# Audio tower on one core: a new order of calls on all five engines, and the low parts cut in two

## The reference, cut to what matters

```python
def _L0_tok_ref(user_batch, filt, W_k, b_k):      # B=32, L=256, D=128, F=8 -> 248 tokens of 64
    windows = user_batch[:, idx, :]
    out = jnp.einsum('blfd,fd,fdk->blk', windows, filt, W)
    return jax.nn.relu(out + b_k)
...
    q = src @ Wq.T + bq; k = src @ Wk.T + bk; v = src @ Wv.T + bv
    row_mask = (q[:, :, 0] != 0) & (k[:, :, 0] != 0)
    prob = softmax(where(row_mask, q @ k.T / 8, -1e9)); prob = where(row_mask, prob, 0)
    return (prob @ v) @ Wo.T + bo
...
    topk_vals, topk_idx = jax.lax.top_k(x @ Wg + bg + bias, 2)     # 8 experts, 2 chosen
    h = relu(x @ W1[e] + b1[e]); y = h @ W2[e] + b2[e]             # all 8 experts, hidden 128
    out = sum_e combine[:, e] * y[e]
...
h = _L0_tok_ref(x, ...)
h = h + _L0_attn_ref(_layernorm(h), ...)
h = h + _L0_ffn_ref(_layernorm(h), ...)
```

## Time and profile before

| | us |
|---|---|
| median of 3 runs | 327.02 (326.04 to 329.09) |
| the profiled execution, device time | 325.06 |
| its span, first to last instruction | 323.3 |
| mean granted TensorE clock | 0.988 of full speed |

### The profile page before, as it was taken

How to read it: one execution, slowest core, us unless ns; L and a number is a source line. 1 busy time by engine, 2 the same in 40 slices (tenths; PEclk the granted TensorE clock), 3 DMA queues, 4 the chain that set the end, 5 groups by cost and what they waited for, 6 DMA issues and landing times.

```text
span 323.3 us, 5597 instructions
## 1 busy us (share of the span) xinstructions
PE 287.1 (89%) x1486; PEld 188.3 (58%) x1486; DVE 253.1 (78%) x824; ACT 230.7 (71%) x545; POOL 96.6 (30%) x85
## 2 busy tenths in 40 slices
PE   8767879899999989898999999898999997978783
PEld 7545647576565748575665657484756654554340
DVE  2476777979798888889797987888897988886653
ACT  2357687878686977978686969869786869574541
POOL 1112141414234241614142241515142312213113
PEclk9789999999999999999999999999999999999999
DMA  5311215061432525170624334251605133232241
GB/s 176 101 32 34 66 52 139 4 177 31 119 89 83 129 81 128 20 190 4 160 51 105 103 81 129 79 131 37 154 22 140 36 87 90 81 95 80 66 128 31
DMA packets 17248, 28.61 MB, mean 88 GB/s; under 512 B 3265, under 2 KB 13761, under 8 KB 17217
## 3 DMA queue, kind: packets, MB, share of 16 engines
q1 hardware_dynamic: 16928, 27.98, 32.8%
q10 hardware_dynamic: 288, 0.28, 0.2%
HBM read 21.90 MB, written 2.29 MB: 75 GB/s over the span
## 4 chain that ended last, share of the span: by engine, by line
PE 76%; issue 7%; DVE 6%; ACT 3%; DMA 3%; SPq 2%; POOL 1%; POOLq 0%; DVEq 0%; ACTq 0%
PE bank_y L877 15%; PE bank_a L817 11%; PE bank_h L867 10%; PE bank_h L868 8%; PE bank_s L926 4%; PE bank_s L845 4%; PE bank_s L834 4%; PE bank_s L909 3%; PE bank_b L886 3%; PE bank_b L935 2%; PE bank_s L882 2%; PE bank_b L882 2%; PE bank_s L886 2%; PE bank_s L957 2%; PE bank_s L946 2%
## 5 line engine op out<-in xcount | busy, mean ns | idle before, releaser
L380 ACT ACTIVATE hid<-bank_h,col 128x496 f32<-128x496 f32 x128 | 82.3, 672 | 17.4 <-PE bank_h L868 17.1
L867 PE MATMUL bank_h<-xs,w_hi 128*128 128x496 f32 x128 | 59.4, 464 | 9.6 <-issue 7.5
L877 PE MATMUL bank_y<-hid,w_sb 128*64 128x496 f32 x256 | 60.4, 587 | 3.1 <-issue 3.1
L331 POOL TENSOR_TENSOR p<-p,rmask 124x496 f32<-124x496 f32 x32 | 32.4, 1013 | 77.6 <-DVE rmask L585 77.5
L255 POOL TENSOR_TENSOR total<-acc 128x496 f32<-128x496 f32 x16 | 20.0, 1250 | 110.3 <-DVE acc L569 110.3
L569 DVE SCALAR_TENSOR_TENSOR acc<-bank_y,col,cb 128x496 f32<-128x496 f32 x64 | 45.0, 722 | 7.8 <-DMA cb<-weights 6.1
L868 PE MATMUL bank_h<-xs,w_lo 128*128 128x496 f32 x128 | 49.5, 387 | 0.0
L867 PEld LDWEIGHTS bank_h<-xs,w_hi 128*128 128x128 f32 x128 | 24.1, 188 | 27.9 <-issue 24.0
L371 ACT ACTIVATE p<-bank_s,nmax 124x248 f32<-124x248 f32 x64 | 29.4, 469 | 9.7 <-DVE nmax L576 9.7
L877 PEld LDWEIGHTS bank_y<-hid,w_sb 128*64 128x64 f32 x256 | 16.6, 136 | 29.1 <-issue 26.1
L338 POOL TENSOR_TENSOR x_lo<-x,x_hi 128x512 fp32r<-128x512 f32 x16 | 24.4, 1524 | 29.3 <-ACT x_hi L436 29.3
(11 more groups left out here) (105 smaller groups left out, 563.2 us busy)
## 6 DMA issues: line engine op xcount, KB each, us to landing
cb<-weights SPq DMA_DIRECT2D x64, 248.0 KB, 3.9
kk<-kk SPq DMA_DIRECT2D x16, 248.0 KB, 3.1
x<-xt SPq DMA_DIRECT2D x15, 256.0 KB, 3.9
out<-h SPq DMA_DIRECT2D x16, 124.0 KB, 2.2
w_sb<-w SPq DMA_DIRECT2D x3, 256.0 KB, 3.9
wtok_sb<-wtok SPq DMA_DIRECT2D x1, 256.0 KB, 2.7
x<-xt ACTq DMA_DIRECT2D x1, 256.0 KB, 4.0
weights<-ct_sb SPq DMA_DIRECT2D x16, 15.5 KB, 1.4
```

Of the source, the lines that this page charges most:

```text
L331: pool.tensor_tensor(p_sb[b][0:HALF, :, :], p_sb[b][0:HALF, :, :], rmask[0:HALF, b, :].unsqueeze(2).to_broadcast([HALF, 2, WIN]), ALU.mult ...
L380: act.activation(hid[2 * (p % 2) + s][:, :], bank_h[s][:, 0:TOK], ACT.Relu, bias=col[:, C_B1 + e:C_B1 + e + 1]).then_inc(hid_ready[s], 1)
L867: pe.matmul(bank_h[e % 2][:, 0:TOK], w1_hi[:, e, :], xs[m % 2][:, :], start=True, stop=False)
L877: last = pe.matmul(bank_y[p % 2][s * D:s * D + D, 0:TOK], w2_sb[:, 2 * p + s, :], hid[2 * (p % 2) + s][:, :], start=True, stop=True)
```

## The change

The formulas, the tiles and the number of instructions stay. What changes:
- `low_parts` becomes `low_part(…, b)`, one instruction for a call, and the two halves are called apart. `tlo` and `xlo` now count 2 for a group, and those who wait for them wait for 2.
- `recip` is cut in two calls (`recip`, `masked_recip`), `denominator` too (`index_values`, `denominator`); `weights` and `second_weight` become one.
- DVE: `low_tokens_2(n, 0)` stands between `largest` and `difference`; `low_tokens_2(n, 1)` between `both_weights` and `masked_recip(c, 0)`. `masked_recip(c, 1)`, `low_tokens(d, 0)`, `weigh(m, 3)`, `low_tokens(d, 1)` follow one another. `weigh(n, 0)` and `weigh(n, 1)` both stand ahead of `normalise_2`.
- POOL: `low_inputs` comes first; `scale`, `scale`, `add(pool, m, 2)` stay in that order.
- ACT: `exps(c, 0)`, `exps(c, 1)` side by side, `relu(m, 7)` ahead of them.
- PE: `hidden(m, 4)` moves behind the first two convolution passes, `values` between two hidden layers, the last two convolution passes between `hidden(n, 1)` and `turn_p(c, 0)`, `turn_p(c, 1)` behind `hidden(n, 3)`; at the end comes expert pair 0, attention, fold, pair 1.
- SP: both halves of `spread` follow each other, inputs are loaded three iterations ahead of `t`, and `copy_keys` comes after the spreads.

The groups are renamed by one: `a, d, c, n, m = t+1, t, t-1, t-2, t-3`. The new lists of ACT, DVE and PE are shown here in full, one call on a line and without the tests for live groups; the old ones stand in the listing above.

```diff
@@ -237,12 +237,13 @@
         def run(iteration):
-            for t in range(-1, GROUPS + 4):
+            for t in range(-3, GROUPS + 3):
                 iteration(t)
-        def low_parts(eng, dst, src):
-
-            eng.tensor_tensor(dst[D:128, 0:WIN], src[0:D, :], dst[0:D, 0:WIN].bitcast(F32), ALU.subtract)
+        def low_part(eng, dst, src, b):
+
+            if b == 0:
+                return eng.tensor_tensor(dst[D:128, 0:WIN], src[0:D, :], dst[0:D, 0:WIN].bitcast(F32), ALU.subtract)
             return eng.tensor_tensor(dst[0:D, WIN:TOK], src[D:128, :], dst[D:128, WIN:TOK].bitcast(F32),
                                      ALU.subtract)
@@ -303,19 +304,19 @@
                 sp.dma_start(out[f], h2[f % 3][:, :]).then_inc(o_out[f % 3], 16)
             def iteration(t):
-                c, m, f = t - 1, t - 3, t - 4
-                if live(f):
-                    spread(f, 1)
-                if live(t + 1):
-                    if t + 1 > 0:
-                        load(t + 1)
-                if live(m):
-                    store_weights(m)
-                    spread(m, 0)
-                if live(f):
-                    store(f)
-                if live(c):
-                    copy_keys(c)
+                d, c, n, m = t, t - 1, t - 2, t - 3
+                if live(t + 3):
+                    if t + 3 > 0:
+                        load(t + 3)
+                if live(n):
+                    spread(n, 0)
+                    spread(n, 1)
+                if live(d):
+                    copy_keys(d)
+                if live(c):
+                    store_weights(c)
+                if live(m):
+                    store(m)
             run(iteration)
             for i in range(3):
@@ -339,16 +340,16 @@
                                    ALU.subtract).then_inc(xl_ready, 1)
             def iteration(t):
-                n, f = t - 2, t - 4
-                if live(f):
-                    add(pool, f, 1)
-                if live(n):
-                    scale(n, 0)
-                    scale(n, 1)
-                if live(f):
-                    add(pool, f, 2)
-                if live(t + 1):
-                    low_inputs(t + 1)
+                a, c, m = t + 1, t - 1, t - 3
+                if live(a):
+                    low_inputs(a)
+                if live(m):
+                    add(pool, m, 1)
+                if live(c):
+                    scale(c, 0)
+                    scale(c, 1)
+                if live(m):
+                    add(pool, m, 2)
             run(iteration)
@@ -456,55 +457,54 @@
     act.activation(eg[0:HALF, :], dlt[0:HALF, :], ACT.Exp).then_inc(eg_ready, 1)
     def iteration(t):
+    a, d, c, n, m = t + 1, t, t - 1, t - 2, t - 3
     turned(n, 1)
+    relu(m, 3)
     high_queries(c)
     high_keys(c)
+    high_inputs(a)
+    rectify(d)
     square(n, 1, bank_s[0])
     relu(m, 4)
     log_variance(n, 1, bank_s[0])
     inverse_deviation(n, 1, xn2_ready)
     square(d, 0, bank_b)
+    high_tokens_2(n)
     relu(m, 5)
     relu(m, 6)
     log_variance(d, 0, bank_b)
     gate_exp(n)
+    relu(m, 7)
     inverse_deviation(d, 0, xn_ready)
+    exps(c, 0)
+    exps(c, 1)
+    high_tokens(d)
+    relu(n, 0)
+    relu(n, 1)
+    later_taps(a)
+    relu(n, 2)
+    turned(c, 0)
     run(iteration)
...
@@ -580,6 +580,8 @@
                 dve.wait_ge(ex_ready, 2 * n + b + 1)
                 after(dve, p_ready, 2 * n + b - 1)
                 dve.reciprocal(rsum[0:HALF, b, :], psum_p[0:HALF, b, :]).then_inc(rs_ready, 1)
+
+            def masked_recip(n, b):
                 dve.wait_ge(rs_ready, 2 * n + b + 1)
                 dve.wait_ge(mask_ready, n + 1)
                 dve.tensor_tensor(rmask[0:HALF, b, :], rsum[0:HALF, b, :], mask[0:HALF, :, b],
...
@@ -711,14 +714,14 @@
                                          in1=kmask[0:HALF, :, :], op0=ALU.not_equal,
                                          op1=ALU.mult).then_inc(mask_ready, 1)
-            def low_tokens(c):
+            def low_tokens(c, b):
                 dve.wait_ge(thi, c + 1)
-                low_parts(dve, ts, xn).then_inc(tlo, 1)
-
-            def low_tokens_2(n):
+                low_part(dve, ts, xn, b).then_inc(tlo, 1)
+
+            def low_tokens_2(n, b):
                 dve.wait_ge(xhi, n + 1)
-                low_parts(dve, xs[n % 2], xn2).then_inc(xlo, 1)
+                low_part(dve, xs[n % 2], xn2, b).then_inc(xlo, 1)
             def residual(n):
@@ -733,64 +736,71 @@
     dve.tensor_tensor(h2[f % 3][:, :], bank_s[1][:, 0:WIN], h2[f % 3][:, :], ALU.add).then_inc(out_ready, 1)
     def iteration(t):
+    a, d, c, n, m = t + 1, t, t - 1, t - 2, t - 3
+    normalise_2(n)
     keep_values(c)
     masks(c)
     logits(n)
     largest(n)
+    low_tokens_2(n, 0)
     difference(n)
     indices(n)
     rowmax(c, 0)
+    index_values(n)
     denominator(n)
+    one_hot(n)
+    rowmax(c, 1)
+    weights(n)
+    normalise(d)
+    recip(c, 0)
+    both_weights(n)
+    low_tokens_2(n, 1)
+    masked_recip(c, 0)
+    keep_weights(n)
+    recip(c, 1)
+    weigh(m, 2)
+    masked_recip(c, 1)
+    low_tokens(d, 0)
+    weigh(m, 3)
+    low_tokens(d, 1)
+    value_weights()
+    both_taps(a)
+    attention_parameters()
+    add(dve, m, 3)
+    residual(c)
+    final(m)
+    low_queries(d)
+    low_keys(d)
+    expert_parameters()
+    weigh(n, 0)
+    weigh(n, 1)
     run(iteration)
...
@@ -861,7 +871,7 @@
                 if e == 0:
                     pe.wait_ge(xhi, m + 1)
-                    pe.wait_ge(xlo, m + 1)
+                    pe.wait_ge(xlo, 2 * m + 2)
                 after(pe, hid_ready[e % 2], 4 * m + e // 2)
                 pe.matmul(bank_h[e % 2][:, 0:TOK], w1_hi[:, e, :], xs[m % 2][:, :], start=True, stop=False)
@@ -929,7 +939,7 @@
             def queries_keys(c):
                 pe.wait_ge(thi, c + 1)
-                pe.wait_ge(tlo, c + 1)
+                pe.wait_ge(tlo, 2 * c + 2)
                 after(pe, ct_ready, c - 1)
                 pe.matmul(bank_b[:, 0:TOK], wqk_hi[:, :], ts[:, :], start=True, stop=False)
...
@@ -963,64 +973,68 @@
     centre(n, 1, bank_s[0], h2[n % 3])
     def iteration(t):
+    a, d, c, n, m = t + 1, t, t - 1, t - 2, t - 3
+    conv(a, range(0, 2))
+    hidden(m, 4)
+    variance(n, 1, bank_s[0])
+    first_centre(d)
+    hidden(m, 5)
+    values(c)
+    hidden(m, 6)
+    conv(a, range(2, 4))
+    gate(n)
+    variance(d, 0, bank_b)
+    conv(a, range(4, 6))
+    scores(c, 0)
+    hidden(m, 7)
+    scores(c, 1)
+    conv(a, range(6, 8))
+    conv(a, range(8, 10))
+    expert_out(m, 2)
+    expert_out(m, 3)
+    turn_weights(n)
+    hidden(n, 0)
+    hidden(n, 1)
+    conv(a, range(10, 12))
+    turn_p(c, 0)
+    hidden(n, 2)
+    hidden(n, 3)
+    turn_p(c, 1)
     parameter_products()
+    queries_keys(d)
+    expert_out(n, 0)
+    attend(c)
+    fold_halves(m)
+    expert_out(n, 1)
+    second_centre(c)
     run(iteration)
```

More of the change, by code:

```diff
@@ L679, in normalise_2 @@
                 after(dve, gate_done, n)
-                after(dve, xlo, n)
+                after(dve, xlo, 2 * n)
                 dve.tensor_tensor(xn2[:, :], bank_s[0][:, 0:WIN], rstd[1][:, :], ALU.mult).then_inc(xn2_ready, 1)
@@ L735, in iteration @@
             def iteration(t):
-                d, c, n, m, f = t, t - 1, t - 2, t - 3, t - 4
-                if live(c):
-                    normalise(c)
-                if live(m):
-                    one_hot(m)
-                if live(n):
-                    rowmax(n, 1)
-                if live(m):
-                    weights(m)
-                    second_weight(m)
-                if live(n):
-                    recip(n, 0)
-                if live(m):
-                    both_weights(m)
-                    low_tokens_2(m)
-                if live(n):
-                    recip(n, 1)
-                if live(m):
-                    keep_weights(m)
-                if live(f):
-                    weigh(f, 2)
-                    weigh(f, 3)
-                if live(c):
-                    low_tokens(c)
-                    if c == 0:
-                        value_weights()
-                if live(f):
-                    add(dve, f, 3)
-                    final(f)
-                if live(d):
-                    both_taps(d)
-                    if d == 0:
-                        attention_parameters()
-                if live(n):
-                    residual(n)
-                if live(c):
-                    low_queries(c)
-                    low_keys(c)
-                    if c == 0:
-                        expert_parameters()
-                if live(m):
-                    weigh(m, 0)
+                a, d, c, n, m = t + 1, t, t - 1, t - 2, t - 3
+                if live(n):
+                    normalise_2(n)
                 if live(c):
@@ L781, in iteration @@
                 if live(n):
-                    normalise_2(n)
-                if live(m):
-                    weigh(m, 1)
```

(35 more changed lines are left out.)

111 lines of the change are left out of this document (62 added, 49 removed).

## The result

| | before | after |
|---|---|---|
| median, us | 326.53 (324.31 to 329.09, 4 runs) | 308.52 (306.51 to 308.60, 4 runs) |
| profiled execution, us | 325.06 | 308.53 |
| its span, us | 323.3 | 306.7 |

The ratio of the times is 0.9431, with a 95% interval of 0.9351 to 0.9512: 5.7% faster. The prediction said 311 us and a range of 308 to 323 against 327.02. The profiled execution was forecast at 309.1 and took 308.53. The forecast's own ratio, 311 / 327.02 = 0.951, is at the edge of the interval.

The account below looks back on a forecast made before the run. A latency chain through DVE, delayed by POOL's port locks, was taken to set the 17.90 us beat. Waits of 14.3 plus 1.7 at the end give 325.06 - 16.0 = 309.1; with 1.96 for the median, 311 us, range 308 to 323.

Parts of the forecast that it names:

- PE's two gaps: PE idles 0.46 us before the first hidden layer (L867) and 0.40 before the query/key product (L935) each period.
- The beat is a loop through DVE: A chain from centring to gate, DVE's small calls, `xlo` and back over PE sets the 17.90 us beat.
- Who starts first takes the port: DVE's halves of `ts` start 0.04 and 0.06 us ahead of POOL's second scale and second addition, locking POOL out.
- the rival with the lost race: POOL starts ahead of a half of `ts`; PE stalls 0.65 before L935 in place of 0.40: 322 us, chance 0.20.
- the size of the two waits: PE's waits before L867 and L935 add up to 7.5 + 1.5 + 5.3 = 14.3 us, all gained.
- the forecast 3.98: Start of the gate behind the second centring: 3.52 before, plus 0.46 for one more hidden layer ahead of it.
- PE can give 0.86 at most: PE is busy 17.04 of each 17.90 us beat, so at most 0.86 can be gained; said within the another-wait rival.
- 14.3 - 10.3 + 1.7: The 1.7 is the gain taken from 3.1 us that second expert pairs wait once the convolution has run out.
- the 1.96 between the profiled execution and the median: The median of the runs lies 327.02 - 325.06 = 1.96 us above the profiled execution; added to 309.1.
- The transfers just fit: The second transfer of `cb` lands after 3.9 to 5.2 us; DVE's following calls end at 2.7 to 4.0, gate at 3.98.
- the likeliest case: The forecast itself, 311 us, with its own range of 308 to 315; chance 0.55.

Follow-up runs that it names:

- the second experiment: The changed kernel with one small DVE memset put between `masked_recip(c, 1)` and `low_tokens(d, 0)`: 320.74 us, ratio 0.9841 to the kernel before.

## What the prediction had right, and where it failed

- *PE's two gaps are waits for `xlo` and `tlo`*: right. One lock put back at either place brings a wait back there, in all nine periods from 80 to 230 us.
- *The beat is a loop through DVE, not PE's own*: right. With DVE's old stretch in the new kernel it stayed at 17.86.
- *Who starts first takes the port, with leads of 0.04 and 0.06*: right, and close: the trace has 0.05 and 0.04, the same in all twelve periods. The Trainium skill's rule ("SBUF — State Buffer", "SBUF: two separate sides") agrees, and so does the one on held instructions ("VectorE: DVE Perf Modes", "Two Vector instructions with no wait between them"): the half starts at 162.33, 0.03 behind the mask's end at 162.15 + 0.15. Had DVE been 0.05 later, the rival with the lost race would have come, and the second experiment shows its time, 320.74, for which I had 322. To forecast leads of that size from starts read to 0.01 took some luck.
- *First step that failed: the size of the two waits, taken as 14.3 us.* I took PE's waits from the brackets and from the waits view, 0.46 + 0.40 = 0.86 a beat. A bracket counts from the end of the record before, and that lies behind the point at which the next instruction could have started. I had L867 wait for the end of `turn_weights`, 0.28 behind its start (9.76), and L935 3.46 behind that (13.22). In the period from 134.51 they came at 9.63 and 12.77 (144.14 and 147.28), 0.45 sooner.

  L857 to L867 was 0.74 with a bracket of 0.46; freed, it is 144.14 - 144.10 = 0.04, so the wait was 0.70. From L867 to L935 it was 3.40; now it is 3.14 with two more convolution passes of 0.46 in it, a gain of 0.72 where the bracket said 0.40.

  Two parts of that can be told apart. The passes ahead of L935 start 0.22 to 0.23 apart (170.10, 170.32), so L935 could have started at 170.32 + 0.23 and waited 0.57. The other 0.15 or so lies in the two turnings of p, 0.87 together before (168.69 to 169.56, and POOL's second scale ended at 169.10) and 0.35 each after.

```profile
168.69 1.11 PE L845 MATMUL bank_s<-cst,p 124*124 124x124 f32 x8
169.56 0.47 PE L867 MATMUL bank_h<-xs,w_hi 128*128 128x496 f32 x1
...
170.10 0.39 PE L867 MATMUL bank_h<-xs,w_hi 128*128 128x496 f32 x1
170.32 0.39 PE L868 MATMUL bank_h<-xs,w_lo 128*128 128x496 f32 x1
```

- *The beat's 1.31 adds up.* As means of the twelve beats, with the passes that changed places taken off: 0.60 from L857 to L867, 0.73 from there to L935, 0.13 from there to the centring; less 0.10 from the centring to the gate (4.08 in place of the forecast 3.98) and 0.05 from the gate to the second expert pairs.
- *For the same reason "PE can give 0.86 at most" was wrong*: the busy 17.04 of 17.90 contains the tails of records in front of each wait.
- *What I left out: the ends.* I took the start at no change, and it lost 1.4 us; the tail lost 1.7. Both go with a lower granted clock. Why the clock fell there in one execution and not in another stays open.
- *The near total was luck.* The brackets give 10.3 us in the twelve beats, which gained 15.8; everything else was forecast at 14.3 - 10.3 + 1.7 = 5.7 and gave 3.9 - 1.4 - 1.7 = 0.8. The two errors were of opposite sign, which is why the sum for the profiled execution (16.0, measured 16.6 between the spans) came so near.
- *Second step that failed: the 1.96 between the profiled execution and the median.* I carried it over from the kernel before. After the change the profiled execution, 308.53, is the median, 308.52. That is 2.0 of the 2.5 us by which the median misses 311. The profiled execution of before was simply one of its faster ones.
- *The transfers just fit*: right in most periods. The landing took longer than before, which had 3.9 and at most 5.2:

```profile
DMA to landing us min/median/max: 3.5/4.7/5.7
```

DVE waited 0.91 and 0.96 us ahead of `weigh` in two of the twelve periods, and these two beats were 16.8 rather than 16.5. What came of it is told in the last section.
- *The range* reached down to 308 only, the low end of the likeliest case, and the result lies on that edge.

## What to carry to other kernels

Where POOL reads SBUF, look at every DVE instruction with two SBUF inputs beside it, short ones too, and put it a few hundredths of a microsecond ahead of POOL's start or beside nothing; PSUM-reading instructions such as `weigh` go into POOL's shadow. After every move look at all such pairs again, not only at the one that was moved. Cure a lock only together with the order on the engine that waits for POOL's result, or the wait moves there. Measure a wait on PE as the distance between starts, held against the same distance without the wait, and not by the idle bracket; take off what else changed between the two starts.

## What the runs showed of the hardware

- The lead needed is tiny. DVE's 0.05 us decided each of the twelve periods the same way; a DVE instruction of 0.11 us turned it, and there POOL was first by 0.01 (167.07 and 167.08).
- POOL's next instruction doesn't keep the port: DVE's second half came in between two POOL instructions with a start 0.04 us ahead of the second one (163.54 and 163.58).
- A DVE instruction with one SBUF input can be held as well. In the kernel after, `kmask` (124 x 4) takes 0.66 us instead of 0.17 when POOL's first addition is under way (154.63 to 155.88), in two of its sixteen:

```profile
155.25 0.66 DVE L710 TENSOR_SCALAR kmask<-v_sb 124x4 f32<-124x4 f32 x1
```

- That did cost something. The two are the periods in which DVE had waited 0.91 and 0.96 us for `cb`, so that `kmask` fell beside the addition. There `logits` starts 4.99 and 5.04 us behind the centring in place of 4.62, the first hidden layer 0.29 and 0.36 behind L867 in place of 0.04, and the beat is 16.76 and 16.81 in place of 16.47. Without the 0.49 of the hold `logits` would have been in time (5.04 - 0.49 = 4.55).
